# An audio-tower block on one Trainium2 core: at the end one of each quad's three tiles is scaled by ScalarE and added by GpSimd

## The reference

```python
vals, idx = jax.lax.top_k(g, K)                 # K = 4 of 16 experts
w = jax.nn.softmax(vals, axis=-1) / K
full_w = zeros((T, E)).at[arange(T)[:, None], idx].set(w)
...
y = jnp.einsum('tei,eih->teh', h, w2) + b2
out = jnp.einsum('teh,te->th', y, full_w) * K
return x + out
```

## Time and profile before

| | us |
|---|---|
| median of 3 runs | 805.38 |
| lowest and highest run | 803.54, 806.48 |
| the profiled execution | 803.8 |
| its span | 802.0 |

### The profile page before, as it was taken

One profiled execution on the slowest core, in us unless ns is written; L12 is line 12 of the kernel. 1 busy time (PEld: TensorE's weight loads), 2 busy tenths in 40 slices (PEclk: granted clock), 3 DMA queues, 4 the chain that ended last, 5 costly groups with the idle time before them and its releaser, 6 DMA issues. The chain is left out here.

```text
span 802.0 us, 16019 instructions
## 1 busy us (share of the span) xinstructions
PE 409.9 (51%) x4141; PEld 280.2 (35%) x4142; DVE 624.2 (78%) x1840; ACT 548.3 (68%) x916; POOL 436.3 (54%) x546
## 2 busy tenths in 40 slices
PE   0277545554535445435354221110999999999400
PEld 0133213232322323213123220110787778778300
DVE  3686578989898887988979973644798889889378
ACT  0235389999978969879698762216898889889300
POOL 9443263836355566755855765435266556656600
PEclk9989655555555555555555555555899999999755
DMA  8469999697202020020000011102344434333095
GB/s 183 47 145 321 319 318 297 199 287 219 57 1 84 20 74 30 24 73 20 25 29 29 15 47 48 43 28 82 89 127 125 119 118 121 109 110 97 1 382 197
DMA packets 102400, 93.47 MB, mean 117 GB/s; under 512 B 14822, under 2 KB 96493, under 8 KB 102338
## 3 DMA queue, kind: packets, MB, share of 16 engines
q1 hardware_dynamic: 88938, 72.87, 32.9%
q0 software_dynamic: 10272, 17.70, 6.4%
q10 hardware_dynamic: 3128, 2.16, 0.9%
HBM read 35.21 MB, written 61.24 MB: 120 GB/s over the span
## 5 line engine op out<-in xcount | busy, mean ns | idle before, releaser
L677 POOL DMA_INDIRECT expert_rows<-stage,dest x118 | 116.6, 988 | 85.9 <-DVE dest L1398 64.6
L617 POOL DMA_INDIRECT region<-rows,slots x60 | 62.1, 1035 | 28.4 <-issue 15.1
L1470 PE MATMUL pX<-arena,WA 128*128 128x384 f16 x86 | 35.3, 514 | 74.1 <-ACT arena L762 50.0
L641 POOL CAST oq<-o 128x384 bf16<-128x384 int8 x24 | 21.4, 892 | 75.8 <-ACT o L830 75.6
L532 POOL TENSOR_TENSOR w1s<-stage,w1s 128x384 f16<-128x384 f32 (+8 forms) x72 | 57.6, 800 | 6.4 <-ACT w1s L735 1.4
L1689 PE MATMUL pX<-w2s,stage 128*128 x472 | 56.6, 250 | 4.4 <-ACT stage L898 2.6
L1577 PE MATMUL pP<-idb,S_p 128*88 128x128 bf16 x192 | 25.8, 315 | 57.0 <-DVE S_p L1238 57.0
L617 POOL DMA_INDIRECT region<-arena,slots x36 | 37.3, 1036 | 18.3 <-issue 8.5
L904 ACT ACTIVATE stage<-arena 128x512 f16<-128x512 f32 x59 | 37.2, 630 | 13.2 <-DVE arena L1394 12.1
L1285 DVE SCALAR_TENSOR_TENSOR S_e<-S_sq,kf,S_pow 128x1056 f32<-128x1056 f32 x24 | 35.4, 1477 | 11.6 <-ACT S_sq L844 11.4
L605 POOL CAST arena<-arena 128x384 bf16<-128x384 int8 x42 | 28.0, 673 | 29.8 <-ACT arena L762 29.5
(11 more groups left out here) (365 smaller groups left out, 1749.0 us busy)
## 6 DMA issues: line engine op xcount, KB each, us to landing
region<-zrow SPq DMA_DIRECT2D x45, 800.0 KB
arena<-region SPq DMA_DIRECT2D x59, 200.0 KB
w1s<-expert_rows SPq DMA_DIRECT2D x16, 384.0 KB, 7.7
stage<-in_L_ffn_w_dram SPq DMA_DIRECT2D x24, 192.0 KB
stage<-in_L_ffn_w_dram SPq DMA_DIRECT2D x8, 384.0 KB
w2s<-expert_rows SPq DMA_DIRECT2D x8, 384.0 KB, 13.7
arena<-in_x_dram SPq DMA_DIRECT2D x4, 672.0 KB
expert_rows<-stage,dest POOLq DMA_INDIRECT x118
```

What stands on the lines that cost most here:

```text
L617: pool.indirect_dma_start(region_rows, bass.IndirectOffsetOnAxis(ap=slots[q % 3][:, i, m:m + 1], axis=0), rows[q % 3][:, i, :].bitcast(I16 ...
L677: pool.indirect_dma_start(y_dram, bass.IndirectOffsetOnAxis(ap=dest[(st - 7) % 8][:, j:j + 1], axis=0), ysb[b][:, j, :], None, bounds_chec ...
L1470: ins = pe.matmul(bank[:, 0:384], W[:, 128 * c:128 * c + 128], xT[:, kind, :], start=kind == 0, stop=kind == 2)
```

## The change

DVE's loop over the tiles of a quad runs over two in place of three. The third tile (`n = 3q + 2`) is handled by two other engines. ACT multiplies the four expert rows of that tile by their weights, in place in `ybuf`, by four activations (Identity, per-partition scale), each of which increments `scaled`. POOL then adds the scaled rows to `xsel` one after the other with `tensor_tensor`, each add waiting for `scaled` and for the add before it (`added`). ACT's store of a quad waits for DVE's 8 instructions and POOL's 4 adds, and stands in ACT's program after the scaling of the next quad.

```diff
@@ POOL, after step_slots(pool, ...)
+            pool.wait_ge(s["base_ready"], NT)
+            for q in range(NQ):
+                for m in range(TOPK):
+                    n = 3 * q + 2
+                    pool.wait_ge(s["scaled"], TOPK * q + m + 1)
+                    if m:
+                        pool.wait_ge(s["added"], TOPK * q + m)
+                    pool.tensor_tensor(xsel[:, n, :], ybuf[n][:, C * m:C * m + C], xsel[:, n, :], ALU.add).then_inc(s["added"], 1)
@@ ACT, after step_slots(act, ...)
-            for q in range(NQ):
-                act.wait_ge(s["combined"], TOPK * 3 * (q + 1))
+            def scale_rows(q):
+
+                act.wait_ge(y_loaded[q], 48)
+                for m in range(TOPK):
+                    n = 3 * q + 2
+                    act.activation(ybuf[n][:, C * m:C * m + C], ybuf[n][:, C * m:C * m + C], ACT.Identity,
+                                   scale=W4[:, n, m:m + 1]).then_inc(s["scaled"], 1)
+
+            def store_rows(q):
+
+                act.wait_ge(s["combined"], TOPK * 2 * (q + 1))
+                act.wait_ge(s["added"], TOPK * (q + 1))
                 row = 4 * KEEP * q
...
+            act.wait_ge(s["weights_ready"], 1)
+            for q in range(NQ):
+                scale_rows(q)
+                if q:
+                    store_rows(q - 1)
+            store_rows(NQ - 1)
@@ DVE, the combination
             for q in range(NQ):
                 for m in range(TOPK):
-                    for i in range(3):
+                    for i in range(2):
                         n = 3 * q + i
                         if m == 0:
                             dve.wait_ge(y_loaded[q], 48)
                         else:
-                            dve.wait_ge(s["combined"], TOPK * 3 * q + 3 * m - 2 + i)
+                            dve.wait_ge(s["combined"], TOPK * 2 * q + 2 * m - 1 + i)
```

More of the change, by code:

```diff
@@ L295, in audio_tower @@
             tp_filled tp_drained h_ready l_done gs_ready a_ready hi_ready lo_ready lot_ready ave_ready te_copied mm2_done y_out dest_ready
-            tails_zeroed rk_done combined out_stored""".split()
+            tails_zeroed rk_done combined scaled added out_stored""".split()
         s = {n: sem(n) for n in names}
```

## The result

The changed kernel takes 807.28 us (median of 20 runs, 805.10 to 811.66) against 804.58 for the kernel before (20 runs, 802.56 to 807.40). The ratio is 1.004, with a 95% interval of 1.0024 to 1.0055: slower by some 3 us (the interval is 1.9 to 4.4). The forecast was +0.3 us.

The account below looks back on a forecast made before the run. DVE's instruction count bounds the combination, above a floor set by loads. 21.1 us for 64 instructions plus 32 x 0.34 for adds gives 32.0 against 31.7, so 805.38 + 0.3 = 805.7 us, range 799.5 to 810.5.

Parts of the forecast that it names:

- the floor: Final combination: loads limit the end however little DVE does; the last quad is in SBUF by 790.3 us.
- the first rival: Combination: POOL and DVE don't disturb each other, so loads bound the end; 5.3 us less, 800.1; 12%.
- ACT costs nothing: Combination: ACT's scaling and stores, 3.2 us a quad, fit in its idle time and cost nothing.
- The turns: Combination: DVE and POOL alternate at SBUF, one instruction each; a held DVE instruction ends 0.21 us after POOL.
- the signs named ahead: Changed profile, 767 to 798: some 8 DVE instructions per 4 us, held ones near 0.75, adds 0.55 to 0.7.
- the third rival: Combination: DVE keeps POOL out, 24 adds follow after DVE; 9.5 us more, 815; sign: only adds far over 0.7; 6%.
- The price of an add: Combination: each of POOL's 32 adds costs DVE 0.34 us, from an add of 0.55 and a gap of 0.08.
- the prediction's own bound of 0.42: Combination: cost to DVE per add if POOL's requests come as late as possible; sum 34.5 us, +2.8.
- late requests: Combination: POOL asks only when DVE's next instruction is all but there, 0.12 us later; an add then costs 0.42.
- POOL never ends a quad last: Combination: POOL finishes each quad's adds before DVE does, 4.4 us after DVE's end two quads earlier.
- The cover that the prediction counted for POOL: Combination: DVE needs two more quads, over 7 us, while POOL's path through stores, scaling and adds takes 4.4.

Follow-up runs that it names:

- experiment 3: Changed kernel with POOL's 32 adds left out, ACT's scaling, waits and stores kept; ratio 0.9945 to the kernel before.
- experiment 6: Changed kernel with each POOL add replaced by a memset that writes SBUF and reads nothing; one run, 800.97 us beside 805.01 for the kernel before.
- experiment 4: Changed kernel with DVE's 16 tiles summed in PSUM, base rows copied there by ACT, POOL's adds kept; ratio 0.994 to the kernel before.
- Experiment 2: Changed kernel with POOL waiting for ACT once per quad, not before each add; ratio 1.0006 to the kernel before.
- experiments 5 and 9: Changed kernel with all loads awaited first and POOL's adds requested at set moments (first add of each quad; every add); 825 and 837 us.
- experiment 7: Changed kernel with DVE starting a quad only after POOL's adds of the quad before; median 806.72 us, ratio 1.0026 to the kernel before.
- the first profile: Profiled execution of the changed kernel from its first measurement, unaltered; 811.65 us, one of its longest.
- experiment 8: Changed kernel run a third time, unaltered; median 806.99 us, ratio 1.003 to the kernel before.
- experiments 1 and 12: Changed kernel run again unaltered, in two sets; ratios 1.0023 and 1.0021 to the kernel before.

## Why the prediction was right, and what it missed

**What bounds the kernel, and the floor: right.** DVE's 64 instructions take 0.41 us each where nothing disturbs them, the loads set the floor at 4.7 to 4.8 us below the kernel before (5.3 was worked out for the first rival), and ACT costs nothing (experiment 3). The forecast time of 805.7 came within 1.6 us of 807.28, but part of that is luck: it stood on 805.38, the median of three runs, where 20 runs gave 804.58. As a difference it was +0.3 against +2.7 to +3.2.

**The turns: right in kind.** DVE and POOL take turns at the SBUF; a held DVE instruction ends 0.21 us after POOL, as in the earlier trace rows. In the turns each finishes one instruction. Of the signs named ahead, the stretches with fewer DVE instructions (6 and 9 in 4 us, some 8 were named), the held ones of 0.74 to 0.81 us and the adds of 0.59 came. For one add the third rival's sign came too: it lasted far longer than 0.7 while DVE's did not.

The Trainium skill ("SBUF — State Buffer", the section on its two separate sides) gives the rule that a VectorE instruction with two SBUF inputs collides only with a GpSimd one that reads SBUF; experiment 6 agrees with that exception (DVE 0.412 beside a memset of 0.418), and experiment 4 with the condition on VectorE.

**The price of an add: the mis-sized term.** The prediction took an add of 0.55, a gap of 0.08, and 0.34 us per add for DVE. Measured are 0.59 for the add, 0.14 for the gap, since each add waits on two semaphores, and (33.5 - 21.1) / 32 = 0.39 per add, which makes DVE's part +1.8 us in place of +0.3. That is inside the prediction's own bound of 0.42, though by POOL's longer beat and not by late requests. Experiment 2 takes the second wait away and gives (32.0 - 21.1) / 32 = 0.34. The rows for the gap came from a chain of instructions with one wait each, and the change had two; that was to be seen in the diff.

**"POOL never ends a quad last": wrong in some executions.** The third rival (DVE keeps POOL out) was priced at 9.5 us from the start of the combination and given 6%. What happens is part of it: POOL gets its turns for five quads, and then in some executions an add is kept out until DVE is done, for 3.4 us. The cover that the prediction counted for POOL, two quads of DVE against 4.4 us, held only as long as each add got its turn. Two of the four profiles of the changed kernel show a kept-out add. Both are of sets near 805 us, and the two without it are of sets near 855, so the chip may have a part in it. The eight of the 20 runs from 809.28 up would fit, but only profiled runs show the add, and one that has it took 808.63. The earlier trace rows showed one case, POOL getting in between two long instructions, and not that POOL always does.

What stays open is what decides it. Both times it was the sixth quad's first add, with DVE at its full beat. In experiments 5 and 9, with no load under way, 23 requests met a DVE instruction with the next directly behind it, and none was kept out for more than one instruction. Some of them came 0.12, 0.14 and 0.16 us after a DVE instruction's start, on either side of the 0.125 and 0.152 of the two kept-out adds. So the moment as the profile shows it doesn't decide by itself. Whether a load under way, the buffers, the chip or a finer moment is needed wasn't shown.

**The sum of it.** The turns make 1.8 us. The ratio of 1.004 is 3.2 us, and the medians differ by 2.7, so 0.9 to 1.4 are left. A kept-out add of 3.4 us in a quarter to two fifths of the executions would make that up. This is a fit: how often it happens wasn't measured, and experiment 7 has two of 12 runs above 809.28 too. Of the 10.6 us that DVE was relieved of, at most 4.8 were to be had before the loads bound; the turns cost DVE 33.5 - 21.1 = 12.4 us and took them all back.

## What to carry to other kernels

Elementwise work that was moved from VectorE to GpSimd didn't run beside VectorE here, where VectorE read two tensors from SBUF and GpSimd read SBUF. A GpSimd add cost VectorE its own length and gap less one VectorE step: 0.39 us for an add whose VectorE version cost 0.33. Count it so first, and measure. Ask first whether one VectorE input can lie in PSUM: 16 copies by an idle engine turned a loss of 0.2 to 0.4% into a gain of 0.6% here. And look for the floor under the engine that bounds (here the loads, 8 us ahead of DVE's end) before counting what relieving it brings.

## What the runs showed of the hardware that was not expected

- A GpSimd add can be kept out by VectorE instructions at a steady beat of 0.329 us for as long as they last: 8.96 and 8.93 us for an add of 0.59 (the first profile and experiment 8). In 23 requests at set moments it didn't occur; what brings it about is open.
- A second semaphore wait ahead of a GpSimd add costs 0.06 to 0.07 us (gap 0.144 against 0.078, step 0.73 against 0.67; experiments 1 and 2).
- The kernel before took 804.6 to 805.4 us on some chips and 852 to 856 on others, with the difference in the steps of the experts. DVE's part of the combination took 33.5 us on both (experiments 1 and 12 on the second kind, 7 on the first).
